# Rsqrt by logarithm, exponential and a Newton step in layer 0, a shorter QR step, LayerNorm products moved to GpSimd, and new positions for the planner

## The reference, cut to what matters

```python
# layer 0; 16 heads of 9 columns
xn = _ln(x) * (1 + sc_msa[:, None, :]) + sh_msa[:, None, :]
q, k, v = split(xn @ w_qkv + b_qkv)
q = _ln(q, g_q); k = _ln(k, g_k)          # over the 9 columns of a head: (z - m) * rsqrt(v + 1e-6)
x = x + g_msa * (softmax(q k^T * HD ** -0.5) v @ w_proj + b_proj)
x = x + g_mlp * (gelu(modulated _ln(x) @ w1 + b1) @ w2 + b2)
# layer 1
U, _ = jnp.linalg.qr(P)                    # P is [144, 64]
R = expm(A(cond))                          # one skew 64x64 matrix for each of the 32 rows of x
x = x + ((x @ U) @ R - x @ U) @ U.T
# layers 2 and 3: modulated LayerNorm, attention, MLP or experts, with gates
```

## Time and profile before

| | us |
|---|---|
| median of 3 runs | 1369.18 |
| lowest and highest | 1365.66, 1374.56 |
| profiled execution | 1369.59 |
| its span, first to last instruction | 1367.7 |
| mean granted TensorE clock in it | 0.97 |

### The profile page before, as it was taken

The page is one execution under the profiler, slowest core; times in us unless marked ns, Lnnn a source line. Parts: engine busy times, 40 slices in busy tenths (PEclk is TensorE's granted clock), DMA queues, the critical chain, the costliest instruction groups (busy, mean ns, idle before and its releaser), DMA issues. The chain is left out here.

```text
span 1367.7 us, 36454 instructions
## 1 busy us (share of the span) xinstructions
PE 1285.6 (94%) x13444; PEld 1069.1 (78%) x13444; DVE 957.7 (70%) x2820; ACT 910.3 (67%) x1792; POOL 666.9 (49%) x782
## 2 busy tenths in 40 slices
PE   8898989999999999998999999999999999999998
PEld 7467767777788877676877778778888889888897
DVE  6788788878888746688677777776666656655341
ACT  3664867757767636666776775677867776776641
POOL 5757788988988321132333333244353342515331
PEclk9999989989899899999899999999999999999999
DMA  6321111111121101143121222221111111111100
GB/s 187 95 86 31 44 43 44 47 37 43 37 60 48 54 24 44 45 124 79 59 69 58 65 64 67 58 77 42 37 57 35 53 42 48 53 34 58 44 12 22
DMA packets 98069, 76.15 MB, mean 56 GB/s; under 512 B 25536, under 2 KB 83179, under 8 KB 97766
## 3 DMA queue, kind: packets, MB, share of 16 engines
q1 hardware_dynamic: 97894, 73.83, 19.0%
HBM read 43.27 MB, written 28.95 MB: 53 GB/s over the span
## 5 line engine op out<-in xcount | busy, mean ns | idle before, releaser
L1788 PE MATMUL p_B<-s_pC,s_H 128*128 128x144 f32 x1900 | 250.4, 288 | 0.9 <-ACT s_FA L1020 0.8
L1408 DVE TENSOR_REDUCE s_MX<-p_S 128x16 f32<-128x2048 f32 x96 | 219.4, 2286 | 38.6 <-PE p_S L1720 37.6
L1788 PEld LDWEIGHTS p_B<-s_pC,s_H 128*128 128x128 f32 x1900 | 239.9, 190 | 7.0 <-issue 2.0
L1117 ACT ACTIVATE s_Pm<-p_S 128x2048 f32<-128x2048 f32 x96 | 180.2, 1878 | 25.1 <-PE p_S L1734 24.5
L962 POOL TENSOR_TENSOR s_s<-s_s,s_half 128x32 f32<-128x32 f32 x32 | 175.0, 5471 | 17.2 <-DVE s_s L1376 16.9
L1168 ACT ACTIVATE s_H<-p_B,s_pC 128x512 f32<-128x512 f32 (+1 forms) x207 | 137.8, 686 | 61.5 <-PE p_B L1654 60.2
L958 POOL TENSOR_TENSOR s_OC<-s_OC,s_RB 72x256 f32<-72x256 f32 x96 | 70.6, 736 | 191.1 <-DMA s_RB<-sums 191.0
L1519 DVE SCALAR_TENSOR_TENSOR s_CQ<-p_B,s_rw,s_CQ 128x144 f32<-128x144 f32 x128 | 41.1, 363 | 115.1 <-PE p_B L1788 114.5
L966 POOL TENSOR_TENSOR s_X<-s_X,s_GA 128x144 f32<-128x144 f32 x96 | 48.5, 505 | 138.2 <-DVE s_GA L1427 138.1
L1660 PE MATMUL p_B<-s_eye,s_QK 128*128 128x128 f32 x768 | 111.1, 282 | 2.8 <-ACT s_JS L1199 1.0
L1660 PEld LDWEIGHTS p_B<-s_eye,s_QK 128*128 128x128 f32 x768 | 88.3, 144 | 15.2 <-issue 5.3
(11 more groups left out here) (318 smaller groups left out, 3214.8 us busy)
## 6 DMA issues: line engine op xcount, KB each, us to landing
heads<-s_OT SPq DMA_DIRECT2D x96, 256.0 KB, 2.3
s_GM<-gates SPq DMA_DIRECT2D x48, 144.0 KB, 3.2
s_GA<-gates SPq DMA_DIRECT2D x96, 72.0 KB, 3.0
s_OC<-heads SPq DMA_DIRECT2D x192, 36.0 KB
s_RB<-sums SPq DMA_DIRECT2D x192, 36.0 KB
s_QT<-s_MS SPq DMA_DIRECT2D x192, 8.0 KB
s_SG<-in_main SPq DMA_DIRECT2D x33, 72.0 KB, 2.2
out<-s_X SPq DMA_DIRECT2D x8, 288.0 KB, 3.6
```

The costliest lines, as they stand in the source:

```text
L1117: e.activation(Pm[n % 2][:, :], bank["s2", i][:, :], ACT.Exp, scale=SCALE).then_inc(SEM["ex"], 1)
L1408: e.tensor_reduce(MX[n % 2][:, :], bank["s1", i][:, :].rearrange("p (h k) -> p h k", h=NH), AX.X, ALU.max, negate=True).then_inc(SEM["mx"], 1)
L1788: ins = e.matmul(bk[:, 256 * i2:256 * i2 + C], hb[0:n, c, 128 * t:128 * t + 128], w2[l][0:n, 5 * x + c, :], start=(c == 0), stop=(c == 4))
```

## The change

**n1 and n2 of layer 0.** DVE's n1 only sums the squares (line 1376 is gone). ACT gets a step n1: logarithm of sum / 9 + EPS, then the exponential of -0.5 times that, both 128x32. POOL's n1 is gone. DVE's n2 puts a Newton step for the inverse root in front, three linked scalar_tensor_tensor operations of 128x32. ACT also takes the logarithm of one element before its first exponential and, in layer 0, before the first ex or n1 that follows a run of Gelu.

**QR.** VS and T1 lie in one tensor, TV, so that one strided operation reaches the pivots of both. ACT squares first (scaled by 0.5) and copies after it. POOL's power waits for the square alone and writes SH. DVE's q1 makes the signs as +-0.5, the dot product, and both pivots times the sign; q2 makes both corrected sums in one two-column operation. The signs and the factors 0.25 and 4 go into qm, once.

**LayerNorm.** In layer 0, POOL writes the first 128 columns too, attention's and the MLP's; in layers 2 and 3 all stays. The waits for DVE's part drop out in layer 0.

**Squarings.** POOL's doubling (line 1003) takes its factor from a column of `half` rather than an immediate.

**Planner.** Every layer's positions now run from one value at its first tile to another at its last (`lean`), and all constants have new values. The fixed surcharge SHARED for a port that DVE and POOL share gives way to a flag: such an operation on DVE waits, in the model, for the end of one on POOL. The logarithm counts as a user of the exponential's table. One constant of the model of PE's clock, by which the hum is placed, has a new value.

```diff
@@ planner: costs
-        more = {ACT.Exp: 95, ACT.Gelu_apprx_tanh: 110, ...}[func]
-        return self.part(80 + more + 0.78 * cols(o), {ACT.Exp: "exp", ACT.Gelu_apprx_tanh: "gelu"}.get(func))
+        more = {ACT.Exp: 95, ACT.Ln: 95, ACT.Gelu_apprx_tanh: 110, ...}[func]
+        return self.part(80 + more + 0.78 * cols(o), {ACT.Exp: "exp", ACT.Ln: "exp", ACT.Gelu_apprx_tanh: "gelu"}.get(func))
...
+        if p.shared and e == "dve":
+            ns += max(0.0, taken - now)
+        elif p.shared:
+            taken = now + ns
@@ planner: positions
-TILE = {..., "n1": (-0.683, 3.714, 10.374), "n2": (-0.114, 4.8, 4.506),
+TILE = {..., "n1": (-0.74, -0.678, 2.848, 1.771, 12.768, 13.461), "n2": (0.248, 0.24, 6.629, 5.571, 4.711, 9.48),
...
+    def lean(pos, l, part):
+        return pos[2 * l] + (pos[2 * l + 1] - pos[2 * l]) * part
...
-        s = START["qr"] + START["qr step"] * k
+        s = START["qr"] + START["qr step"] * k - START["qr early"] * max(0, 10 - k)
@@ POOL
-            def normal_rest(bs, MV, VE, XH, done):
+            def normal_rest(bs, MV, VE, XH, done, whole):
                 for k, b in enumerate(bs):
+                    if whole:
+                        e.tensor_scalar(XH[:, k, 0:128], X[:, b, 0:128], MV[:, k, 0:1], VE[:, 1, k:k + 1], ALU.subtract, ALU.mult)
...
-                elif stage == "n1":
-                    n = i[0]
-                    w.wait_ge(*at("n1", n))
-                    e.tensor_tensor(s32[n % 2][:, 3, :], s32[n % 2][:, 2, :], half[:, :], ALU.pow).then_inc(SEM["n1p"], 1)
...
                 elif stage == "q1":
-                    w.wait_ge(*at("qc", i[0], 1))
-                    e.tensor_tensor(sc[:, 1:2], sc[:, 0:1], halfp[0:64, :], ALU.pow).then_inc(SEM["qp"], 1)
+                    w.wait_ge(*at("qc", i[0]))
+                    e.tensor_tensor(SH[:, i[0]:i[0] + 1], sc[:, 0:1], halfp[0:64, :], ALU.pow).then_inc(SEM["qp"], 1)
...
-                    e.tensor_scalar(SC[:, r, 0, :], HS[:, r, :], 2.0, None, ALU.mult).then_inc(SEM["sqs"], 1)
+                    e.tensor_scalar(SC[:, r, 0, :], HS[:, r, :], half[:, 33:34], None, ALU.mult).then_inc(SEM["sqs"], 1)
@@ ACT
             w.wait_ge("d_first", 48)
+            e.activation(lnz[:, :], eye[0:1, 0:1], ACT.Ln)
             e.activation(ex1[:], condT1[:], ACT.Exp, scale=-1.0).then_inc(SEM["sil_a"], 1)
...
+            gelu = False
             for stage, i in steps["act"]:
+                if stage == "ue":
+                    gelu = True
+                elif stage in ("ex", "n1") and gelu:
+                    gelu = False
+                    if i[0] < B and not isinstance(e, Probe):
+                        e.activation(lnz[:, :], eye[0:1, 0:1], ACT.Ln)
...
+                elif stage == "n1":
+                    n = i[0]
+                    s = s32[n % 2]
+                    w.wait_ge(*at("n1", n))
+                    w.wait_ge("d_small", 32)
+                    e.activation(s[:, 1, :], s[:, 0, :], ACT.Ln, bias=half[:, 32:33], scale=1.0 / HD).then_inc(SEM["n1l"], 1)
+                    w.wait_ge(*at("n1l", n))
+                    e.activation(s[:, 3, :], s[:, 1, :], ACT.Exp, scale=-0.5).then_inc(SEM["n1p"], 1)
...
+                    e.activation(JS[:, 0:C - k], bank["qb", i][0:64, 0:C - k], ACT.Square, scale=0.5, accum_out=sc[:, 0:1]).then_inc(SEM["qc"], 1)
                     e.copy(VS[:, 0:C - k], bank["qb", i][0:64, 0:C - k]).then_inc(SEM["qc"], 1)
-                    e.activation(JS[:, 0:C - k], bank["qb", i][0:64, 0:C - k], ACT.Square, accum_out=sc[:, 0:1]).then_inc(SEM["qc"], 1)
@@ DVE
-                elif stage == "xh":
+                elif stage == "xh" and i[0] >= B // 2:
...
-                    link(e.tensor_reduce(s[:, 0, :], CS2[:], AX.X, ALU.add))
-                    after()
-                    e.tensor_scalar(s[:, 2, :], s[:, 0, :], 1.0 / HD, EPS, ALU.mult, ALU.add).then_inc(SEM["n1"], 1)
+                    e.tensor_reduce(s[:, 0, :], CS2[:], AX.X, ALU.add).then_inc(SEM["n1"], 1)
...
+                    link(e.scalar_tensor_tensor(s[:, 2, :], s[:, 3, :], -0.5 / HD, s[:, 3, :], ALU.mult, ALU.mult))
+                    after()
+                    link(e.scalar_tensor_tensor(s[:, 2, :], s[:, 0, :], HD * EPS, s[:, 2, :], ALU.add, ALU.mult))
+                    after()
+                    link(e.scalar_tensor_tensor(s[:, 3, :], s[:, 2, :], 1.5, s[:, 3, :], ALU.add, ALU.mult))
+                    after()
...
-                elif stage == "mxh":
+                elif stage == "mxh" and i[0] >= NG:
...
-                    link(e.tensor_tensor_reduce(JK[:, 0:n], T1[:, k:C], VS[:, 0:n], 1.0, 0.0, ALU.mult, ALU.add, sc[:, 6:7]))
-                    e.tensor_scalar(sc[:, 2:3], VS[:, 0:1], 0.0, 2.0, ALU.is_ge, ALU.mult).then_inc(SEM["q1"], 1)
+                    link(e.tensor_scalar(SG_[:, k:k + 1], VS[:, 0:1], 0.0, 0.5, ALU.is_ge, ALU.subtract))
+                    sign = chain[0]
+                    link(e.tensor_tensor_reduce(JK[:, 0:n], T1[:, k:C], VS[:, 0:n], 0.25, 0.0, ALU.mult, ALU.add, sc[:, 1:2]))
+                    w.wait_ge("dseq", sign)
+                    e.tensor_scalar(sc[:, 2:4], TV[0:64, 0:C + k + 1:C + k], SG_[:, k:k + 1], None, ALU.mult).then_inc(SEM["q1"], 1)
...
-                    link(e.scalar_tensor_tensor(SH[:, k:k + 1], sc[:, 2:3], -1.0, sc[:, 1:2], ALU.add, ALU.mult))
-                    after()
-                    link(e.scalar_tensor_tensor(sc[:, 4:5], VS[:, 0:1], SH[:, k:k + 1], sc[:, 0:1], ALU.mult, ALU.add))
-                    link(e.scalar_tensor_tensor(sc[:, 6:7], T1[:, k:k + 1], SH[:, k:k + 1], sc[:, 6:7], ALU.mult, ALU.add))
+                    link(e.scalar_tensor_tensor(sc[:, 4:6], sc[:, 2:4], SH[:, k:k + 1], sc[:, 0:2], ALU.mult, ALU.add))
```

## The result

The changed kernel takes 1443.4 us (median; 1439.3 to 1446.9) against 1367.4 us of the kernel before on the same chip (1361.6 to 1374.6). The ratio is 1.055, its 95% interval 1.049 to 1.061: 76 us slower, 62 us above the predicted 1381 and beyond the end of the range at 1404.

The account below looks back on a forecast made before the run. Layer 0 was taken to have no single bound, layer 3 to be bound by PE. The sum was 1369.6 + 13 (ACT in layer 0) - 2 (transition) + 0 (planner), about 1381 us, range 1332 to 1404.

Parts of the forecast that it names:

- the loads: ACT, layer 0: logarithm and exponential each need a table load per tile, 72 us for 28 tiles.
- one table for both: Rival, layer 0: one table serves logarithm and exponential, DVE sets the length, 1340 us (1320 to 1356); chance 0.24.
- How full can ACT get?: Layer 0, 50 to 450 us: ACT fills to 89.5%, so the stretch takes 413 us, +13 us (-25 to +45).
- The "bound" of +45 us at 83%: Layer 0, upper limit: ACT gets only as full as DVE is now, 83%, so the stretch takes 445 us.
- where PE idles the hum grows: PE, layer 0: behind a late ACT, PE waits for copies and fills idle time with dummy matmuls; no size given.
- an order made for another sum: Rival, layer 0: planner's fixed order ignores the logarithm's loads, ACT fills to only 83%, +45 us, 1413 us; chance 0.14.
- the planner at nothing, -15 to +10: All layers: changed positions and planner costs reorder the steps, taken as 0 us, bounds -15 to +10.
- DVE and POOL, terms of no weight: Layer 0, 50 to 450 us: POOL falls from 320 to about 192 us, DVE from 333 to 313.
- no single bound among the helpers: Layer 0: no engine alone sets the length; DVE (333 of 400 us) is fullest in real work.
- The transition (-2 us): Into layer 2: a shorter QR chain helps the last steps, limited by an equally late path, -2 us (0 to -3).
- Layer 3 within 3 us of today's: Layer 3, 850 to 1300 us: PE is full (443.6 of 450 us), so its length stays within 3 us.

Follow-up runs that it names:

- one_table: The changed kernel, same order, loading one table that holds both logarithm and exponential in place of the one-element logarithm: median 1372.6 us, ratio 1.0058 to the kernel before.
- load_ex3: one_table plus 32 loads of its table, one behind the exponential ex of each layer 3 tile, order unchanged: ratio 1.0119 to the kernel before.
- Experiment 4: Kernel before's order kept on every engine, layer 0's roots moved to ACT, with no, 32 or 62 added table loads: ratios 0.9954, 1.0224, 1.0605.
- old_order_one: The kernel before with layer 0's roots on ACT and one table, its order kept on every engine: median 1363.4 us, ratio 0.9954.
- loads_planned: The changed kernel, still loading two tables in turn, with the planner giving the logarithm its own table so the loads count: ratio 1.0515 to the kernel before.
- load_n1: one_table plus 32 loads of its table, one per layer 0 tile between n1's logarithm and exponential, order unchanged: ratio 1.0121 to the kernel before.
- load_ex0: one_table plus 32 loads of its table, one behind the exponential ex of each layer 0 tile, order unchanged: ratio 1.0230 to the kernel before.
- one_table_06: one_table with the planner's old constant 0.6 in place of 0.7 in its model of PE's clock: ratio 1.0191 to the kernel before.

## Why the prediction was wrong, step by step

**Right: the loads.** Two loads a tile, 1.283 us each, beside the one that the one-element logarithm brings. The prediction had about 74 for 28 tiles; the profile shows 65 in 50 to 450 us, where some 26 tiles now fit. The rival "one table for both" was false for this kernel as it was written. The Trainium skill (page "ScalarE: Activation LUTs", section "Table sets: the hidden batching unit") counts one load for a logarithm and the exponential after it; the 26 and 20 loads at L1124 and L1122 say otherwise for the changed kernel, and one_table says that such a table exists and serves both once it is the one that is loaded. Even then the time was 1372.6, not the rival's 1340.

**Wrong, and the cause of the miss: "How full can ACT get?"** The prediction let ACT fill to 89.5% before the stretch lengthens, and so gave 91 us of new work on ACT a price of 13 us. ACT filled to 82% of 50 to 450 us and 78% of layer 0 (417 of 536). A share is not what gives out. In the changed kernel's own order the loads cost 68 us (one_table), where the step had 13 for them and the operations together. ACT's operations stand in a fixed queue on the way of PE's banks, and a load delays everything behind it. How much of that comes back later is not told by ACT's share: little in layer 0 (0.85 of the loads' length was paid in one order, 1.1 in the other), about four fifths in layer 3, where ACT was fuller (78% in load_ex3) and PE busy 96%. That the fixed queue is what carries the delay is argued from the chain and the waits; that the loads cost this time is measured. Experiment 4 has the price in layer 0: 0.76 (by the spans) to 0.9 (by the ratios) of a load's length for the first 32, 1.1 for all 62, with ACT at 69 to 73% of the stretch throughout. The engine with the most real work (DVE, 83%) said nothing of this, if, as argued here, the price is set by the delay in ACT's queue. The "bound" of +45 us at 83% was no bound, because it too was a share. Of the 91 us, the prediction's own 77 us of loads at 0.85 (68 of 79.5, one_table) to 1.1 give 65 to 85 us and a sum of 1433 to 1453. The other 14 us, the operations themselves, cost nothing that shows (old_order_one: ACT +13 us in layer 0, the stretch 487 us as before), though that is a net with the power that left POOL.

**Wrong: "where PE idles the hum grows".** It can't: the hums are written into PE's order before the kernel runs. All three kernels of experiment 4 carry the same PE instructions in layer 0. Where PE waits longer than the model thinks, it stays idle, and in the same stretches the granted clock fell from 0.94 to 0.86, so that the same matmuls took 43 us longer. The sum had no term for this, though the earlier trace rows show a clock of 0.93 in this stretch against 0.99 in layer 3.

**The rival "an order made for another sum"** gave 1413, 30 us too low, and had the direction. Its sign came true: ACT stayed below 89%, filled like DVE to 82%. One half of its mechanism fits experiment 4, that in a fixed order the loads cost time while ACT idles elsewhere. The other half, that the order fails since the planner didn't know of the loads, is open. Once the planner counts them nothing is gained (loads_planned, 1.0515), but that kernel also got an order for which no constants were fitted, and such orders lost 8 to 87 us by themselves.

**Too narrow: the planner at nothing, -15 to +10.** one_table, in the changed kernel's order without its loads, stands inside these bounds: +8 us by the ratio, +3 in the profiled execution (layer 0 11 us shorter, layer 2 17 longer, layer 3 6 shorter, the rest 4 longer). This is partly luck: layer 2 alone moved by more than the upper bound, and layer 0 offset it. So as the net of the new order and the new work without their loads the term held. As a bound for an order it was far off: the same work lay 8 and 47 us higher for 10 ns in one planner cost, and 87 us higher under the new constants.

**DVE and POOL, terms of no weight.** Groups of the changed kernel, 50 to 450 us, answer to the earlier trace rows:

```profile
L963 POOL TENSOR_SCALAR s_XHA<-s_X,s_MVA,s_VEA 128x128 f32<-128x128 f32 x26 | 21.9, 841 | 8.8 <-PE p_B L1751 8.6
...
L1608 DVE TENSOR_SCALAR s_scq<-s_T,s_GO 64x2 f32<-64x2 f32 x48 | 15.2, 316 | 0.0
L1615 DVE SCALAR_TENSOR_TENSOR s_scq<-s_scq,s_SH 64x2 f32<-64x2 f32 x48 | 11.7, 243 | 1.8 <-POOL s_SH L1027 0.9
...
L1429 DVE SCALAR_TENSOR_TENSOR s_s<-s_s 128x32 f32<-128x32 f32 x26 | 5.3, 204 | 23.0 <-ACT s_s L1124 23.0
```

The product took 0.84 us (0.66 predicted, inside its bounds), the two-column product with the sign 0.316 (0.141, priced by a row without a second operand from memory), the two-column sum 0.243 (0.257), a Newton operation 0.20 (0.27). DVE's 23 us of waiting at L1429 are new: n2 waits for the exponential and its load. POOL stood at 187 us (192 predicted), in part by luck: the dearer product was offset by 46 of them in the stretch, not 54. In the old order none of it paid: POOL lost 162 us of work between the kernel before and old_order_one (346 to 184 us in layer 0), while ACT gained 13, and layer 0 took 487 us as before. With a new order made for it the sum of all relief shows as the 11 us of one_table's layer 0. That part of the argument, no single bound among the helpers, was right.

**The transition (-2 us)** can't be told apart: in layer 0 of the changed kernel everything is late, the last QR step too (525 us, 482 before).

**Layer 3 within 3 us of today's** held for the changed kernel (422 against 425 us).

## A version that beats both

old_order_one takes 0.9954 of the kernel before (0.9919 to 0.9989), 6 us less, and 82 us less than the changed kernel. It has the roots on ACT with one table, and neither the new QR step nor the moved products nor new positions. The gain is small, under the 1% that the prediction called no change, but its interval lies below 1. That the edit made it isn't shown: in the profiled executions layer 0, the one place where the work differs, takes 487 us in both, and 5 of the 6 us lie in layers 2 and 3, where both kernels run the same instructions in the same order.

## What to carry to other kernels

Don't price an addition to an engine that others wait for by the room that its busy share leaves. Where no engine is the single bound, take its whole length as the first case: in layer 0 ACT at 70% had little room for 1.3 us twice a tile, and in the old order all loads together cost 1.1 of their length while PE's clock fell from 0.94 to 0.86. Where another engine is full, most of it can be hidden: in layer 3 about a fifth was paid. Where the profile can't say whether two functions share a table, take both cases at the full price, for the answer was worth 68 us here and one line of code decided it. And before a loss is put down to changed work in a kernel whose order comes from a fitted planner, hold the order fast and change only the work: 10 ns in one planner cost moved this kernel by 47 us.

## What the runs showed of the hardware

- A load of the table that is already there costs the same 1283 ns as any other (load_n1, load_ex0, load_ex3).
- With the table loaded by hand that holds both, a 128x32 logarithm takes 326 ns and the exponential behind it 231 ns, and no load appears at either.
- PE's granted clock over layer 0, at one list of instructions, was 0.94, 0.91 and 0.86 as ACT's work rose from 338 to 374 and 414 us, and the mean of the same 768 squaring matmuls rose from 280 to 312 ns. With more hum the clock of layer 2 stood at 0.96 in one_table_06, against 0.91 in one_table, and the layer was not shorter.
